# Audio tower on one core: q and k of the attention in two fp32r parts in place of three bf16 ones, with two heads stacked on 64 partitions each

## The reference, cut to what matters

```python
h = tok(x)                                  # [8, 744, 256]: concat of 3 shifted rows @ W.T + b
xn = layernorm(h)
k, q, v = heads(Wk), heads(Wq), heads(Wv)   # 16 heads of 16 columns each
att = einsum('bhqd,bhkd->bhqk', q, k) / sqrt(16)
att = softmax(where(causal, att, -inf))
h = h + einsum('bhqk,bhkd->bhqd', att, v) @ Wp.T + bp
...
h = h + moe(layernorm(h))                   # 4 experts of 1024, top 2, exact gelu
```

## Time and profile before

| | us |
|---|---|
| three runs | 2224.6, 2228.3, 2240.8 (median 2228.3) |
| the profiled execution | 2221.6, span 2219.8 |
| in it: start and first batch's front, to the first `st` | 134.8 |
| the eight batches, first `st` to last `st` | 134.8 to 1414.6, 160 a batch |
| the end of the attention phase | 1415 to 1499 |
| expert phase | from 1500 |

### The profile page before, as it was taken

The page is one execution under the profiler, slowest core; times in us unless marked ns, Lnnn a source line. Parts: engine busy times, 40 slices in busy tenths (PEclk is TensorE's granted clock), DMA queues, the critical chain, the costliest instruction groups (busy, mean ns, idle before and its releaser), DMA issues. The chain is left out here.

```text
span 2219.8 us, 33416 instructions
## 1 busy us (share of the span) xinstructions
PE 1609.7 (73%) x10648; PEld 1223.6 (55%) x10648; DVE 1080.0 (49%) x3362; ACT 710.4 (32%) x1463; POOL 850.1 (38%) x956
## 2 busy tenths in 40 slices
PE   4387586586676676676676586506999989989896
PEld 4254254254254254354354252206999988889886
DVE  1165456446446445555455465023555555555553
ACT  0023333333333333333343353201333333333332
POOL 4314234434524524523523525230444334334434
PEclk9578798789699689699689796658999999999998
DMA  2433524623522632542642543138443443444342
GB/s 85 86 67 90 118 48 109 135 54 94 132 71 85 137 76 73 138 88 73 135 91 69 135 86 95 29 86 290 168 167 142 172 178 131 165 174 170 133 165 81
DMA packets 159549, 256.26 MB, mean 115 GB/s; under 512 B 35092, under 2 KB 127182, under 8 KB 155024
## 3 DMA queue, kind: packets, MB, share of 16 engines
q1 hardware_dynamic: 135760, 217.01, 35.4%
q0 software_dynamic: 23616, 37.12, 5.5%
HBM read 173.92 MB, written 75.29 MB: 112 GB/s over the span
## 5 line engine op out<-in xcount | busy, mean ns | idle before, releaser
L585 ACT ACTIVATE prob<-stb 124x496 f32<-124x496 f32 (+2 forms) x832 | 398.6, 504 | 624.2 <-PE stb L906 611.5
L686 DVE CUSTOM_DVE_ANT_0 unused<-mxb,mask_row 124x372 bf16<-124x372 f32 (+4 forms) x768 | 346.8, 483 | 116.1 <-PE mxb L889 114.2
L1300 PE MATMUL yb<-w2p,hp 128*128 x2448 | 345.7, 287 | 51.0 <-DVE yo L1240 51.0
L929 PE MATMUL pvb<-prob,vaug 124*17 124x372 f32 (+2 forms) x2304 | 218.9, 503 | 204.2 <-POOL prob L522 203.9
L1300 PEld LDWEIGHTS yb<-w2p,hp 128*128 128x128 f32 x2448 | 329.5, 192 | 61.5 <-issue 61.5
L889 PE MATMUL mxb<-kst,qst 96*124 96x372 bf16 (+4 forms) x1024 | 331.3, 359 | 35.6 <-DVE mxp L686 27.5
L1287 PE MATMUL l1b<-x2T,w1s 128*128 128x384 f32 x1632 | 342.8, 346 | 2.2 <-DVE x2T L1199 1.2
L906 PE MATMUL stb<-qst,kst 99*124 99x372 bf16 (+4 forms) x1024 | 320.8, 349 | 16.9 <-ACT prob L585 8.1
L1137 ACT ACTIVATE hf<-l1b,b1c 128x384 f32<-128x384 f32 x272 | 158.0, 581 | 402.7 <-PE l1b L1287 391.8
L1287 PEld LDWEIGHTS l1b<-x2T,w1s 128*128 128x128 f32 x1632 | 280.5, 192 | 2.9 <-DVE x2T L1199 1.6
L522 POOL TENSOR_SCALAR_AFFINE_SELECT prob<-prob 124x496 f32<-124x496 f32 x192 | 117.0, 622 | 353.8 <-ACT prob L585 353.4
(11 more groups left out here) (159 smaller groups left out, 1607.7 us busy)
## 6 DMA issues: line engine op xcount, KB each, us to landing
w1s<-ws SPq DMA_DIRECT2D x34, 2048.0 KB, 10.4
qk_s<-parts SPq DMA_DIRECT2D x192, 93.0 KB
kst<-qk_s SPq DMA_DIRECT2D x192, 93.0 KB, 3.3
xg<-xs SPq DMA_DIRECT2D x34, 396.0 KB, 3.3
qst<-qk_s SPq DMA_DIRECT2D x32, 279.0 KB, 5.1
wraw<-in_w_all SPq DMA_DIRECT2D x32, 256.0 KB, 6.0
ws<-whi SPq DMA_DIRECT2D x32, 256.0 KB, 2.8
ws<-wlo SPq DMA_DIRECT2D x32, 256.0 KB, 4.0
```

Of the source, the lines that this page charges most:

```text
L585: act.activation(dst, src, ACT.Exp, scale=DH ** -0.5).then_inc(exp_done, 1)
L686: done = dve.tensor_tensor_reduce(out=unused[:, n % 2, e * w:(e + 1) * w], in0=src, in1=mask_row[:, T - w:T], scale=1.0, scalar=-3.0e38, o ...
L929: done = nc.tensor.matmul(pvb[2 * DH * h:2 * DH * h + DH + 1, s, q0 - s * HALF:q1 - s * HALF], vaug[:, j, HG * (g % NG) + h, :], p, start= ...
L1300: done = nc.tensor.matmul(yb[i][:, 0:D], hp[x][:, n % HPB, 128 * i:128 * i + 128], w2p[w][:, bass.ds(owners[t], 1), m, :], start=(m == 0 a ...
```

## The change

q and k are split in NPART = 2 fp32r parts, with three pairs (top with top, top with rest, rest with top), so ROWS = 3 x 16 = 48. The stacks are fp32r tiles of 128 partitions with two heads side by side: heads 0 and 2 of a group on partitions 0 to 49, heads 1 and 3 on 64 to 113 (SIDE = 64). The negated maximum is split in two rows in place of three. MX and ST are put in another order, so that neighbours in a table lie on different sides, and the last item of MX (four heads in one bank) becomes two of two heads. NMX grows from 27 to 28.

```diff
-K_PARTS = (0, 0, 0, 1, 1, 2)
-Q_PARTS = (0, 1, 2, 0, 1, 0)
+K_PARTS = (0, 0, 1)
 ROWS = DH * len(K_PARTS)
-NPART = 3
+NPART, SIDE = 2, 64
-MX = ([(5, h, 1, s * HALF, HALF) for h in range(HG) for s in range(2)]
+MX = ([(5, h, 1, s * HALF, HALF) for s in range(2) for h in range(HG)]
...
-      + [(1, h, 2, 0, 2 * TT) for h in (0, 2)]
-      + [(0, 0, 4, 0, TT)])
+      + [(i, h, 2, 0, (i + 1) * TT) for i in (1, 0) for h in range(2)])
...
-        kst = [sb(f"kst{g}", [ROWS + NPART, HG, T], bf16) for g in range(NG)]
-        qst = [sb(f"qst{g}", [ROWS + NPART, HG, T], bf16) for g in range(NG)]
+        kst = [sb(f"kst{g}", [128, HG // 2, T], fp32r) for g in range(NG)]
+        qst = [sb(f"qst{g}", [128, HG // 2, T], fp32r) for g in range(NG)]
...
-                pool.memset(kst[g][ROWS:ROWS + NPART, :, :], 1.0).then_inc(consts, 1)
+                pool.memset(kst[g][:, :, :].bitcast(fp32), 1.0).then_inc(consts, 1)
...
-                    if kind == "qk":
-                        pool.wait_ge(qk_evac, a * 8 + n + 1)
-                        pool.tensor_copy(parts[:, n % 2, 1, :], rest[:, n % 2, :]).then_inc(qk_mid, 1)
-                        pool.wait_ge(qk_mid, a * 8 + n + 1)
-                        pool.tensor_tensor(parts[:, n % 2, 2, :], rest[:, n % 2, :], parts[:, n % 2, 1, :],
-                                           ALU.subtract).then_inc(qk_low, 1)
...
-                        dve.tensor_tensor(rest[:, n % 2, :], pab[:, 0:HALF], parts[:, n % 2, 0, :],
+                        dve.tensor_tensor(parts[:, n % 2, 1, :], pab[:, 0:HALF], parts[:, n % 2, 0, :].bitcast(fp32),
...
-                            done = nc.tensor.matmul(out, qst[g % NG][0:ROWS, h + e, TT * i:TT * i + TT],
-                                                    kst[g % NG][0:ROWS, h + e, k0:k0 + w], start=True, stop=True)
+                            side, pair = SIDE * (h % 2), h // 2 + e
+                            done = nc.tensor.matmul(out, qst[g % NG][side:side + ROWS, pair, TT * i:TT * i + TT],
+                                                    kst[g % NG][side:side + ROWS, pair, k0:k0 + w], start=True, stop=True)
...
-                            done = nc.tensor.matmul(out, kst[g][:, h, TT * j:TT * j + TT], qst[g][:, h, q0:q0 + w],
-                                                    start=True, stop=True)
+                            side = SIDE * (h % 2)
+                            done = nc.tensor.matmul(out, kst[g][side:side + ROWS + NPART, h // 2, TT * j:TT * j + TT],
+                                                    qst[g][side:side + ROWS + NPART, h // 2, q0:q0 + w], start=True, stop=True)
```

More of the change, by code:

```diff
@@ L247, in attention_phase @@
         xnT = [sb(f"xnT{p}", [128, KC, T], fp32r) for p in range(2)]
-        parts = sb("parts", [128, 2, NPART, HALF], bf16)
-        rest = sb("rest", [128, 2, HALF])
-        kst = [sb(f"kst{g}", [ROWS + NPART, HG, T], bf16) for g in range(NG)]
-        qst = [sb(f"qst{g}", [ROWS + NPART, HG, T], bf16) for g in range(NG)]
+        parts = sb("parts", [128, 2, NPART, HALF], fp32r)
+        kst = [sb(f"kst{g}", [128, HG // 2, T], fp32r) for g in range(NG)]
+        qst = [sb(f"qst{g}", [128, HG // 2, T], fp32r) for g in range(NG)]
         vaug = sb("vaug", [TT, NT, NH, DH + 1])
@@ L256, in attention_phase @@
         negm = sb("negm", [HG * NT, TT])
-        negr = sb("negr", [HG * NT, TT])
-        negp = sb("negp", [HG * NT, NPART, TT], bf16)
+        negp = sb("negp", [HG * NT, NPART, TT], fp32r)
         prob = {0: sb("prob0", [128, HG, T]), 1: sb("prob1", [128, HG, T - TT]),
@@ L383, in emit @@
                             sp.wait_ge(st_full, to * (NG * NST) + (n + 1 - NG) * NST)
[L384 to L389, removed]
+                        for e in range(2):
+                            for at, t in enumerate(K_PARTS):
+                                sp.dma_start(kst[n][SIDE * e + DH * at:SIDE * e + DH * at + DH, :, :].bitcast(fp32),
+                                             qk_s[to, 0, HG * n + e:HG * n + HG:2, t].rearrange("h r c -> r h c")
+                                             ).then_inc(stack_loaded[n], 16)
+                            sp.dma_start(qst[n][SIDE * e:SIDE * e + 2 * DH, :, :].bitcast(fp32),
+                                         qk_s[to, 1, HG * n + e:HG * n + HG:2].rearrange("h t r c -> (t r) h c")
+                                         ).then_inc(stack_loaded[n], 16)
+                            sp.dma_start(qst[n][SIDE * e + 2 * DH:SIDE * e + 3 * DH, :, :].bitcast(fp32),
+                                         qk_s[to, 1, HG * n + e:HG * n + HG:2, 0].rearrange("h r c -> r h c")
                                          ).then_inc(stack_loaded[n], 16)
@@ L419, in emit @@
                     if kind == "mx_neg":
[L421 to L424, removed]
+                        sp.wait_ge(neg_split, b * (2 * NG) + 2 * (n + 1))
+                        for e in range(2):
+                            for t in range(NPART):
+                                row = SIDE * e + ROWS + t
+                                sp.dma_start(qst[n % NG][row:row + 1, :, :].rearrange("p h (i q) -> p (h i) q", i=NT).bitcast(fp32),
+                                             negp[12 * e:12 * e + 12, t, :].bitcast(fp32)).then_inc(negm_loaded, 16)
                     if kind == "res_load":
@@ L682, in emit @@
                         for e in range(heads):
-                            src = mxb[n % MXB][0:TT, e * w:(e + 1) * w]
-                            top = mxp[:, n // NMX % 2, (h + e) * NT + i, slot:slot + 1]
+                            src = mxb[(b * NG * NMX + n) % MXB][0:TT, e * w:(e + 1) * w]
+                            row = h % 2 * (HG // 2) + h // 2 + e
+                            top = mxp[:, n // NMX % 2, row * NT + i, slot:slot + 1]
                             if k0 + w == (i + 1) * TT:
@@ L1312, in program @@
     r_s = nc.dram_tensor("r_s", [2 * HG * NT, TT], fp32, kind="Internal").ap()
-    qk_s = nc.dram_tensor("qk_s", [NB, 2, NH, NPART, DH, T], bf16, kind="Internal").ap()
+    qk_s = nc.dram_tensor("qk_s", [NB, 2, NH, NPART, DH, T], fp32, kind="Internal").ap()
     ws = nc.dram_tensor("ws", [2 * NE, 128, 2, KC * H], fp32, kind="Internal").ap()
```

37 lines of the change are left out of this document (15 added, 22 removed).

## The result

| | before | after |
|---|---|---|
| median of four runs, us | 2229.1 | 2367.0 (2342.2 to 2375.4) |
| ratio to before, 95% interval | | 1.059 (1.050 to 1.068) |
| span of the profiled execution, us | 2219.8 | 2367.8 |
| mean granted clock | 0.851 | 0.739 |
| first and last exponent (ACT), us | 135.4, 1414.9 | 132.5, 1560.2 |

The account below looks back on a forecast made before the run. It took PE to wait mostly for chains through several engines. Terms -4.5 - 8.8 + 0 - 8 - 7 = -28.3 us, from 2228.3 on the median's footing, gave 2200; range 2162 to 2245.

Parts of the forecast that it names:

- What bounds the kernel: Whole batch: PE nearly full only in the first 24 us, then mostly waiting for chains through several engines.
- The term of `mx` and `st`: Matmuls of `mx` and `st`: side-by-side pairs, fp32r cost and mode changes sum to nothing, bounds -0.5 and +1.5 a batch.
- Mode changes: Full-height product within a stretch of `mx` and `st`: 0.19 us a visit; six at `tok` count, +1.2 us; elsewhere hidden.
- the rival on the other side: Each mode change around full-height products is paid in the open, 35 a batch: 2242; chance 0.19 with its cousin.
- Its point of decision: The rival on the other side decides from about two thirds of its visits in the open on (28 us).
- Its cousin: Short fp32r products of `mx` and `st` run at the plain float32 rate: 42 us, 2242 again; shares the 0.19.
- After a stall: At half clock, side-by-side pairs shorten `mx` and `st` steps: -1.0 us a batch, -8 for eight; bounds 0 and -3.
- The ten neighbours: At s = 10 to 19, ten neighbours on different sides with no `tok` between run side by side: -1.6 us.
- Start: Halved memsets of `kst` let PE's first matmul come sooner: -4.5 us, between 0 and -5.1.
- `qk`: POOL's cast and subtraction go, one store issue is saved twice: -1.25 us a batch, -8.8 for seven; bounds 0 and -3.
- DMA: Stack loads in half as many runs, stores a third more bytes: -1.0 us a batch, -7; bounds +1 and -4.
- fp32r: Matmuls of 372 columns take 0.18 us against 0.16: +0.02 each, +0.4 over twenty of `mx` and `st`.

Follow-up runs that it names:

- the kernel with the twenty products: Changed kernel plus 20 full-height products of 372 columns, their result overwritten, ahead of the first `v` of each batch: 2352.4 us, ratio 1.056 to before.
- PE alone: No score computed; PE runs stretches of full-height, one-sided and two-sided products on loaded data, in two runs, from half and from full clock; no kernel time given.
- the sides apart: Changed kernel with the heads of ST in the order 1, 0, 3, 2, so `mx` and `st` beside `v` stand on different sides: 2335.3 us, ratio 1.046.
- the full-height kernel: Changed kernel with the second side on partitions 48 to 95 and `mx` and `st` contracting over 96 or 98 rows: 2235.5 us, ratio 1.0031.
- the one-sided mixture: Stretch with PE alone: steps of `mx`, `st` (48 rows on one side) and six `v`; 2.48 us a step at half clock, 1.43 at full.
- the second run of PE alone: PE alone, six stretches each behind 20 us of dense full-height fp32r at full clock, in place of starting at half clock; no kernel time given.

## Why the prediction was wrong, by its own steps

**What bounds the kernel.** I read that PE waits for chains and concluded that its speed counts only in few places. But where PE is not full it was at full clock for most of the time; at half clock the first 24 us of a batch have more PE work than time. PE's spare time was conditional on its clock, and I took the clock for given. This is the step that failed. In the sum it stands as the sentence that at `v`, `proj`, `turn` and `qk` the next product waits for ACT or DVE anyway and hides the change of mode. At `v` the wait is gone, PE is busy in 32.5 of 32.5 us, and a step takes 2.58 us in place of 1.52. The term of `mx` and `st` stood at nothing, bounds -0.5 and +1.5 a batch; the mode measured +131 us, some 16 a batch.

**Mode changes.** The mechanism was named, as the rival on the other side. Its price was 0.19 us a visit. Measured it is 0.23 to 0.40 at full clock and 0.58 at half, because the second product behind a change waits as well (0.16 at half). Beside `v` its point of decision, two thirds of the visits in the open, was not what decided: with the clock at full, as in the kernel with the twenty products, they are hidden; with the clock at half they are not. Over the whole batch the rival may be nearer to the truth than my sum: 35 visits at 0.40 to 0.58 us would be an estimated 14 to 20 us. Its cousin was half right, by the records of PE alone: 248 fp32r columns come 0.11 apart, no more than their share of 372, and 124 come 0.11 apart too, twice theirs.

**After a stall** I counted -8: at half clock the pairs would shorten the steps. The sign was wrong. A pair does shorten them (a step of `v` at half clock takes 2.27 us with the sides apart and 2.58 on one side), but beside `v` the one-sided products leave the clock down. The ten neighbours that I counted at s = 10 to 19 are eight by the tables. That the tables put neighbours on different sides I took from the tables, not from the order in which PE meets `mx`, `st` and `v`.

**Start**: -4.5 expected, -2.9 at the first exponent of these two profiles; in the six others with the new start it comes at 130.2 to 134.2, in two more with the old one at 136.3 and 137.6, so the term is not far off, as far as their spread lets one say. POOL is done 5 us sooner, but PE's first matmul now waits for a load, 2.6 us sooner than before:

```profile
3.95 5.52 POOL L465 MEMSET kst<- 128x1488 f32 x4
...
14.88 1.41 PE L795 MATMUL pab<-wr_sb,spare 128*128 128x4 f32 x6 [14.88 <-DMA spare<-in_Wp]
```

**`qk`**: -1.25 a batch expected; in the full-height kernel the stretch from s = 39 to 54 takes 24.4 us in place of 26.3. This step held, but it does not last: from s = 54 to 78 the same kernel takes 43.5 us in place of 41.3.

**DMA**: -1 a batch expected, nothing measured. From the first stack load to ACT's copy it was 107.48 - 89.86 = 17.6 us; in the full-height kernel:

```profile
88.25 1.27 SPq L381 DMA_DIRECT2D kst<-qk_s  x3
...
106.09 0.48 ACT L601 ACTIVATE parts<-pab 128x372 fp32r<-128x372 f32 x1 [15.98 <-DMA qk_s<-parts]
```

That is 17.8 us, and in the median a load of `kst` lands 3.5 us after its issue, 3.3 before. So the longer runs brought nothing here; the prices of a run and of a byte are not shown apart, since the stores and the order changed too.

**fp32r**: I counted 0.02 us each for twenty products. At full clock and in a dense row, PE alone fits 61 fp32r products of 372 columns in 10 us (0.17 from start to start), 65 of bf16 (0.16), and 42 fp32r ones of 124 columns in 4.3 (0.11), twice its columns (0.052). With 256 `mx` and `st` a batch that is an estimated 3 us of PE. It could be a part of why the full-height kernel is at +7 and not at -20, but no run shows it apart, and where PE is fullest, from s = 0 to 21, that kernel's batches are only 0.3 us longer. Its loss stands from s = 54 to 96 (+2.2 and +1.2), where SP folds and loads the stacks; the DMAs and their order are a rival that no run tests.

```profile
34.00:44.00 10.00, 10.00 (x61) 10.00 (x60) 0.00 (x0) 0.00 (x0) 1.00 0.28 98
199.00:209.00 10.00, 10.00 (x65) 8.58 (x64) 0.00 (x0) 0.00 (x0) 1.00 0.01 2
...
458.90:463.20 4.30, 4.30 (x42) 4.30 (x41) 0.00 (x0) 0.00 (x0) 1.00 0.01 4
```

**What stays open.** Beside `v` most of the loss is the clock (6.4 of 7.7 us a batch). For the stretches behind it (+2.6, +7.0, +4.6 us a batch, together more than beside `v`) no run separates the price of the visits from the lower clock; PE alone says that they have both.

## What to carry to other kernels

Before cutting PE's work into halves of the array, look at what keeps its clock up: here the spare time of PE that the profile showed at full clock was gone at half clock, and a change meant to run products side by side lowered the clock of all the others. Put products of half height only where two of them really run side by side, and count the full-height products between them, in the order in which PE meets them and not in the order of a table. A part of a change that is worth having (here half a memset) can be measured alone: its gain is small, 0.3%, and took twelve runs to tell from none.

## What was not expected of the hardware

- PE busy without a gap for 27.8 us (fp32r) and 36.9 us (bf16) on 48 rows of one side stayed at 1.2 GHz; fp32r on two sides went to 2.4. Coming from 2.4 GHz, the dense one-sided stretch fell back (mean 0.55 over 28.2 us), and a mixture with six full-height products a step held (1.00 over 25.3 us).
- With two sides a product can start ahead of one that stands before it in the program: the second `mx` with the first, 0.42 us ahead of the first `st` (870.74 and 871.16 above). The Trainium skill, page TensorE: Matmul & The Clock Gate, section Part 3, has matmuls in program order in start and end; these rows differ for the start.
- Between the 64-row mode and full height 0.10 us goes at full clock and 0.13 at half, and the second product behind the change pays 0.11 or 0.16 again (single starts of the one-sided mixture, 281.7 to 307 us of the second run of PE alone and 298.1 to 337.4 of the first). The Trainium skill, page TensorEngine Tiling, section Key Properties, has the drain, and the trace agrees; the second payment is not in it.
